# Adding the routed experts' rows: fetches that add into the residual, and scatters for the last four tiles

## What is computed

```
scores = softmax(xf @ gate_w)
_, sel = top_k(scores + expert_bias, 2)
order = argsort(sel.reshape(-1), stable=True)
token_idx = order // 2
routed_in = xf[token_idx] * top_scores_sorted[:, None]
h = silu(ragged_dot(routed_in, w1, counts)) * ragged_dot(routed_in, w3, counts)
routed_out = ragged_dot(h, w2, counts)
out = silu(xf @ sw1) * (xf @ sw3) @ sw2
out = out.at[token_idx].add(routed_out)
x = x + tanh(g_ffn[1]) * out
```

## Time and profile before

| what | us |
|---|---|
| median of 3 runs | 1395.21 |
| lowest, highest | 1388.55, 1401.52 |
| the profiled execution | 1396.1 |
| its span | 1394.4 |
| PE busy in it | 1271.6 (91%) |
| DVE, ACT, POOL busy | 652.2, 446.7, 391.7 |

### The profile page before, as it was taken

The page is one execution under the profiler, slowest core; times in us unless marked ns, Lnnn a source line. Parts: engine busy times, 40 slices in busy tenths (PEclk is TensorE's granted clock), DMA queues, the critical chain, the costliest instruction groups (busy, mean ns, idle before and its releaser), DMA issues.

```text
span 1394.4 us, 18292 instructions
## 1 busy us (share of the span) xinstructions
PE 1271.6 (91%) x6256; PEld 1073.6 (77%) x6257; DVE 652.2 (47%) x1103; ACT 446.7 (32%) x755; POOL 391.7 (28%) x327
## 2 busy tenths in 40 slices
PE   4999899999999999999999889995899999998670
PEld 3888778887888888888888778884788888887560
DVE  6555356644366646674555575563123222222116
ACT  3333342333245323531343457421122222221110
POOL 2221111000022302221334231446454310035554
PEclk9999999999999999999999999998899999999785
DMA  6821456544669845965964030435777552257647
GB/s 204 263 84 54 145 210 243 211 159 191 246 216 349 302 181 202 366 239 196 310 226 156 26 84 31 155 117 206 198 222 230 168 141 75 75 181 220 167 145 254
DMA packets 99035, 259.69 MB, mean 186 GB/s; under 512 B 8636, under 2 KB 42648, under 8 KB 86680
## 3 DMA queue, kind: packets, MB, share of 16 engines
q1 hardware_dynamic: 64824, 160.19, 32.4%
q0 software_dynamic: 33680, 98.35, 23.4%
q10 hardware_dynamic: 464, 0.27, 0.1%
HBM read 183.02 MB, written 75.76 MB: 186 GB/s over the span
## 4 chain that ended last, share of the span: by engine, by line
PE 63%; issue 14%; POOL 10%; DMA 7%; DVE 4%; another core or an unknown queue 1%; ACT 1%; POOLq 0%; ACTq 0%; DVEq 0%
PE bank L1145 25%; PE bank L1173 12%; POOL W L592 6%; PE bank L1311 6%; DMA W<-in_L_ffn_w 5%; PE bank L1070 4%; PE bank L1090 4%; PE bank L1346 2%; PE bank L1100 2%; POOL xs_sorted L732 2%; POOL fin_high L761 1%; PE bank L1117 1%; PE bank L1112 1%; DMA wdn<-in_L_ffn_W_down 1%
## 5 line engine op out<-in xcount | busy, mean ns | idle before, releaser
L1145 PE MATMUL bank<-xTh,G 128*128 128x512 f32 x1024 | 279.4, 398 | 1.8 <-DVE xTl L1592 1.8
L1145 PEld LDWEIGHTS bank<-xTh,G 128*128 128x128 f32 x1024 | 189.4, 189 | 42.8 <-issue 3.4
L1311 PE MATMUL bank<-W,dxh 128*128 (+2 forms) x880 | 204.9, 376 | 0.0
L1311 PEld LDWEIGHTS bank<-W,dxh 128*128 128x128 f32 x880 | 171.8, 195 | 15.9
L1173 PE MATMUL bank<-DN,bhh 128*128 128x512 f32 x512 | 157.9, 390 | 0.0
L1311 PE MATMUL bank<-W,dxl 128*128 (+2 forms) x440 | 117.4, 390 | 32.4 <-POOL W L592 16.4
L1145 PE MATMUL bank<-xTl,G 128*128 128x512 f32 x512 | 138.1, 392 | 0.0
L1746 DVE TENSOR_TENSOR dmid<-bank,dsg 128x448 f32<-128x448 f32 x55 | 34.3, 623 | 203.0 <-ACT dsg L954 194.7
L592 POOL TENSOR_TENSOR W<-wst,W 128x1792 fp32r<-128x1792 f32 (+1 forms) x24 | 101.4, 4226 | 87.7 <-DMA W<-in_L_ffn_w 86.3
L1614 DVE SCALAR_TENSOR_TENSOR bs<-bank,tab,bs 128x512 f32<-128x512 f32 x64 | 47.5, 743 | 160.8 <-PE bank L1145 160.8
L1346 PE MATMUL bank<-W,dhh 112*128 (+1 forms) x440 | 114.6, 403 | 0.0
(11 more groups left out here) (247 smaller groups left out, 1961.6 us busy)
## 6 DMA issues: line engine op xcount, KB each, us to landing
G<-gate_up_split SPq DMA_DIRECT2D x48, 1024.0 KB, 7.0
DN<-down_split SPq DMA_DIRECT2D x24, 1024.0 KB, 5.0
wst<-in_L_ffn_w POOLq DMA_DIRECT2D x24, 896.0 KB, 6.2
W<-in_L_ffn_w POOLq DMA_DIRECT2D x24, 896.0 KB, 7.6
gate_up_split<-G SPq DMA_DIRECT2D x16, 1024.0 KB
y_all<-dys SPq DMA_DIRECT2D x55, 256.0 KB
xs_sorted<-zero POOLq DMA_DIRECT2D x3, 3328.0 KB, 21.1
xsd<-xs_sorted SPq DMA_DIRECT2D x39, 256.0 KB, 3.3
```

Of the source, the lines that this page charges most:

```text
L1145: mm = pe.matmul(bank[m][:, :], G[:, c % 2, f, h, m, i, :], a[b % 2][:, i, :], start=(n == 0), stop=(n == 3 * DC - 1))
L1311: mm = pe.matmul(bank[o][:, 0:width], a[par][:, k, :], w[:, bass.ds(slot, 1), at + k * step:at + k * step + width].rearrange("p a n -> p ( ...
```

## The change

1. The last ADDED = 4 routed tiles (t = 51 to 54) are not stored in `y1_dram` any more. ACT writes their results into four of the row buffers (`late`), and at the very end, when all of `out` is stored, POOL adds their rows to `out` in HBM by four indirect scatters with an addition, each of which waits until the one before has landed. A row whose index is out of bounds is left out.
2. So that the rows know their token, each row of `xs1_dram` grows from 512 to 528 elements: behind the 512 stands the token's number plus one. DVE makes the numbers once (`number`), copies 16 columns of them into each row buffer before the row is normalised, and POOL scatters 528 elements. SPq reads the numbers of the last four tiles back (`late_id`), and DVE turns them into indices (`late_i`; rows that hold no token get 4095 and are out of bounds).
3. The 32 fetches of low and high rows add into `xres` themselves (`compute_op=ALU.add`) where they went to `fin_low` and `fin_high`. DVE's 32 additions go. The high fetches now wait for all the low ones. `slr` of a row in the last four tiles points into the zeros of `y1_dram`.
4. The low fetches wait for the tiles before `tlow = min(tend1[6], 35)`; the high fetches for the tiles up to t = 50.
5. The gate is multiplied in by ACT, as it takes a tile out of PSUM (`d_y`), for the shared tiles too; DVE's addition of a shared tile (L1877) becomes a plain one.

```diff
+ADDED = 4
+GATHERED = NT1 - ADDED
+ROW = D + 16
...
+        late = [rows_at[1 + i][:, 0:D] for i in range(ADDED)]
...
+            sp.dma_start(late_id[:, :], xs1_dram[GATHERED * P:NT1 * P, D:D + 1].rearrange("(k p) c -> p (k c)", p=P),
+                         allow_slow_non_contiguous=True).then_inc(s_id, 16)
...
                 load(t + 2)
-                store(t - 2)
-            for t in range(TT + NT1 - 4, TT + NT1):
-                store(t)
+                if t - 2 < TT + GATHERED:
+                    store(t - 2)
 
             for t in range(0, TT, 2):
-                sp.wait_ge(s_x4, t + 2)
+                sp.wait_ge(s_rsc[t // 2], 16 * (2 * TT // 8 + 2))
                 sp.dma_start(out_v[:, t:t + 2, :], xres[:, t:t + 2, :]).then_inc(s_out, 16)
             sp.wait_ge(s_out, 16 * TT // 2)
...
-            last = pool.value_load(tend1_i[0:1, E1 - 2:E1 - 1], min_val=1, max_val=NT1 - 1)
-            half = (last + TT + 1) // 2
+            last = pool.value_load(tlow_i[0:1, 0:1], min_val=1, max_val=GATHERED)
             for i in range(2):
-                pool.wait_ge(s_dst[i], half * 16)
+                pool.wait_ge(s_dst[i], (last + TT + 1 - i) // 2 * 16)
                 alone(None)
+            pool.wait_ge(s_sha, TT)
             for t in range(TT):
-                pool.indirect_dma_start(fin_low[:, t, :], None, y1_dram,
-                                        bass.IndirectOffsetOnAxis(ap=slr[:, 0, t:t + 1], axis=0)).then_inc(s_yg[t % 4], 16)
+                pool.indirect_dma_start(xres[:, t, :], None, y1_dram, bass.IndirectOffsetOnAxis(ap=slr[:, 0, t:t + 1], axis=0),
+                                        compute_op=ALU.add).then_inc(s_yg[t % 4], 16)
             for i in range(2):
-                pool.wait_ge(s_dst[i], 16 * ((TT + NT1 + 1 - i) // 2))
+                pool.wait_ge(s_dst[i], 16 * ((TT + GATHERED + 1 - i) // 2))
+            for i in range(4):
+                pool.wait_ge(s_yg[i], 2 * 16 * TT // 4)
             for t in range(TT):
-                if t >= 8:
-                    pool.wait_ge(s_x4, t - 7)
-                pool.indirect_dma_start(fin_high[:, t % 8, :], None, y1_dram,
-                                        bass.IndirectOffsetOnAxis(ap=slr[:, 1, t:t + 1], axis=0)).then_inc(s_rsc[t % 8], 16)
+                pool.indirect_dma_start(xres[:, t, :], None, y1_dram, bass.IndirectOffsetOnAxis(ap=slr[:, 1, t:t + 1], axis=0),
+                                        compute_op=ALU.add).then_inc(s_rsc[t // 2], 16)
+
+            pool.wait_ge(s_out, 16 * TT // 2)
+            pool.wait_ge(s_slot1, 2)
+            for j in range(ADDED):
+                pool.wait_ge(s_dy, TT + GATHERED + j + 1)
+                wait(pool, s_add, 16 * j)
+                pool.indirect_dma_start(out_rows, bass.IndirectOffsetOnAxis(ap=late_i[:, j:j + 1], axis=0), late[j], None,
+                                        bounds_check=TOK - 1, oob_is_err=False, compute_op=ALU.add).then_inc(s_add, 16)
+            pool.wait_ge(s_add, 16 * ADDED)
...
             def d_y(t):
                 act.wait_ge(s_dd, t + 1)
-                wait(act, s_dst[t % 2], 16 * (t // 2))
-                act.activation(dys[t % 2][:, :], bank[4][:, :], ACT.Copy).then_inc(s_dy, 1)
+                if t < TT + GATHERED:
+                    wait(act, s_dst[t % 2], 16 * (t // 2))
+                act.mul(dys[t % 2][:, :] if t < TT + GATHERED else late[t - TT - GATHERED], bank[4][:, :], gates[:, 3:4]).then_inc(s_dy, 1)
...
+                chain(dve.tensor_scalar(tlow[:, :], tend1[:, E1 - 2:E1 - 1], float(GATHERED), None, ALU.min))
+                chain(dve.tensor_copy(tlow_i[:, :], tlow[:, :]))
...
-                    norm(rows_at[n % 8], xres[:, t, :], t, rsc[:, k, t:t + 1]).then_inc(s_row, 1)
+                    dve.tensor_copy(rows_at[n % 8][:, D:ROW], number[:, t:t + 1].broadcast_to([P, ROW - D])).then_inc(s_row, 1)
+                    norm(rows_at[n % 8][:, 0:D], xres[:, t, :], t, rsc[:, k, t:t + 1]).then_inc(s_row, 1)
```

More of the change, by code:

```diff
@@ L98, in program @@
         gates = keep("gates", [P, 4])
-        zero = keep("zero", [P, P])
+        zero = keep("zero", [P, ROW // 4])
         reset = keep("reset", [P, E1, TT])
@@ L1774, in choice @@
             def choice():
+                chain(dve.tensor_scalar(number[:, :], cst[:, C_THR:C_THR + TT], cst[:, C_LANE:C_LANE + 1], 1.0, ALU.add, ALU.add))
                 for t in range(TT):
@@ L1876, in _ @@
                     dve.wait_ge(s_shl, 16 * (i + 1))
-                    dve.scalar_tensor_tensor(out=xres[:, i, :], in0=row[:, 0, :], scalar=gates[:, 3:4], in1=xres[:, i, :],
-                                             op0=ALU.mult, op1=ALU.add).then_inc(s_sha, 1)
+                    dve.tensor_tensor(xres[:, i, :], row[:, 0, 0:D], xres[:, i, :], ALU.add).then_inc(s_sha, 1)
+                if t == TT + 4:
+                    dve.wait_ge(s_id, 16)
+                    chain(dve.tensor_scalar(late_f[:, :], late_id[:, :], 0.0, 4096.0, ALU.is_equal, ALU.mult))
+                    chain(dve.tensor_tensor(late_f[:, :], late_f[:, :], late_id[:, :], ALU.add))
+                    chain(dve.tensor_scalar(late_f[:, :], late_f[:, :], -1.0, None, ALU.add))
+                    dve.tensor_copy(late_i[:, :], late_f[:, :]).then_inc(s_slot1, 1)
             d_hid(TT + NT1 - 1)
             dve.wait_ge(s_sha, TT)
-            for i in range(4):
-                dve.wait_ge(s_yg[i], 2 * 16 * TT // 4)
-            for t in range(TT):
-                last = dve.scalar_tensor_tensor(out=xres[:, t, :], in0=fin_low[:, t, :], scalar=gates[:, 3:4],
-                                                in1=xres[:, t, :], op0=ALU.mult, op1=ALU.add)
-            chain(last)
-            for t in range(TT):
-                dve.wait_ge(s_rsc[t % 8], 16 * (2 * TT // 8 + t // 8 + 1))
-                dve.scalar_tensor_tensor(out=xres[:, t, :], in0=fin_high[:, t % 8, :], scalar=gates[:, 3:4],
-                                         in1=xres[:, t, :], op0=ALU.mult, op1=ALU.add).then_inc(s_x4, 1)
 def shape_constants():
```

31 lines of the change are left out of this document (16 added, 15 removed).

## The result

| | before | after |
|---|---|---|
| median, us | 1393.39 (4 runs) | 1436.28 (4 runs) |
| lowest, highest | 1388.55, 1401.52 | 1434.38, 1442.96 |
| span of the profiled execution | 1394.4 | 1435.3 |
| ratio after/before, 95% | | 1.0307 (1.0268 to 1.0345) |

The changed kernel is 3.1% slower. The forecast was 1414 us with a range of 1393 to 1428: the direction was right, the size was not, and the range missed it.

What follows compares the result with a forecast made beforehand. PE was taken to dominate the chain unchanged, with POOL's pace and the DMA engines bounding the end. Low fetches 1331.2 to 1359.4, high fetches and stores to 1400.1, scatters to 1412.9 (+18.5): median 1414 us, range 1393 to 1428.

Steps and rivals of the forecast that it cites:

- The stages ahead: Everything before the low fetches: small DVE values and copies ahead of POOL's row scatters add 1.2 us, the rest nothing.
- zeros and numbers: Fill of `xs1_dram`, read of `late_id`, small DVE operations: hidden, 0; the fill under 2 us if its cover went.
- later than 1334: row stage: Sign in the profile after: a first low fetch later than 1334 us means the row tiles' preparation and scatters cost more.
- Row stage: DVE's copies ahead of POOL's row-tile scatters: +0.5 us within a sum of +1.2; as a rival, +6, chance 0.05.
- The start of the low fetches: At the end, low fetches wait for the store of t = 50, not t = 51: 8.57 us earlier.
- The fetches that add: Low and high fetches at the end: each costs 1.58 us of all DMA engines, 0.90 plain plus 0.68 for reading `xres`.
- double or more: Rival on the end's adding fetches: at 1.81 us each the whole takes 1421 us, at 2.7 near 1450; chance 0.15.
- Additions are free: Rival on the end's adding fetches: the second read hides inside POOL's 1.26 us pace, giving 1397 us; chance 0.35.
- 11 us of waiting: Waiting removed at the end: high fetches could start near 1353 rather than 1364 if fetches cost what they did.
- The scatters: Four final scatters in a row, first 3.6 us, others 2.9 each: 12.3, plus 0.2 wait and 0.3 to the span's end.

Runs made afterwards that it cites:

- wide fill: Changed kernel with the zeros of `xs1_dram` written in whole rows of 2112 bytes, not pieces of 528: 1419.38 us, ratio 1.0240.
- late `number`: Changed kernel with DVE making `number` behind the mask that PE waits for, not at the head of `choice`: 1425.04 us, ratio 1.0269.
- both mendings: Changed kernel with the fill in pieces of 2112 bytes and `number` made later on DVE, together: 1413.97 us, ratio 1.0180.

## Why the forecast was right in direction and short in size

*The stages ahead, forecast +1.2.* The first trace had +12.4, the next of the same kernel less: its low fetches start at 1333.28, and the three kernels without the wider rows (1335.50, 1330.89, 1332.63), each less the 8.57 that the change takes from the wait, would start at 1322.3 to 1326.9. So it is 6 to 11 us there, and the traces with the wide fill, alone (1321.39) and with the late `number` (1321.21), have nothing of it left.
- The first step that failed is "zeros and numbers": "the fill of `xs1_dram` is 3% larger and goes while PE is busy", "under 2 us". I counted bytes. The change divides the longer row by four and so makes pieces of 528 bytes, 1.6 times as dear each MB. The cover was the DMA's spare 17 and 30%; it is used up (1.02), and PE's transfers come late. In the first profile that was little, PE short by 0.93 us in 400 to 490; in the four other traces with this fill PE waits 2.7 to 6.1 us for `vnat`, and the rank matmuls start 6 us later in the mean than with the wide fill. The waits lower the clock too: in the windows with waits of 1.93, 2.55, 2.67, 4.63 and 4.67 us the granted clock is 0.91 to 0.97, with those of 0.78 and 1.47 it is 1.00.
- `number` was priced at its own length, 0.2 (it takes 0.23). The price is on PE: the hole ahead of the rank matmuls grows from 1.58 to 1.93 us, the clock falls to its lower level, 32 matmuls take 6.03 and not 3.63 us, and the first scatter comes 4.2 us later. In five profiles with a hole of 1.89 to 1.93 us the clock fell in four; in nine with 1.58 to 1.66 in none. The exception is the kernel with the wide fill alone (1.93, then 3.63), so the longer hole makes it likely and not certain. Mended alone it gave 2.7 us of the median, within the noise.
- Of the first trace's 12.4, the clock is 4.2, the small values ahead of the first scatter 0.5 and PE's waits for the fill 0.9. The rest, some 7, is that execution against before's: 1.2 ahead of the rank matmuls, 2.7 in the row stage, 3.0 behind it, and what held it is not known. By its own sign ("later than 1334: row stage") the forecast was wrong here, but the copies that it meant were not the cause.
- "Row stage", +0.5 for the copies (bounds 0 and 7.6): nothing in seven of the eight profiles with copies. The 49.8 us of the first trace, which would have spoken for a loss of 2.7, is that execution's own. The small values and the first copy ahead of it, priced 0.4 and 0.1, measured 0.5.

*The start of the low fetches, 8.57 us earlier.* Right: with both mendings they start at 1321.21, 9.7 to 14.3 before those of the three kernels that keep the old wait.

*The fetches that add, forecast 1.58 us of the engines, measured 1.80.* This is the second step that failed, a term that was too small: it took the nearest row for the second read and missed by 14%. The rival "double or more" had the price: 2 x 0.90. The Trainium skill's two reads on one ring ("Collectives: The Full Stack", section on why ReduceScatter is half of AllGather) say so of the reductions of collectives, and the trace of the low half agrees: 1.80 us. Beside the stores of `out` it is 1.50, where a plain fetch had 0.483 x 17 / 10.2 = 0.80, a factor of 1.9. But the low half took 34.2 us and not the 31.8 of that rival, because of a term that neither had: POOL's own issue of such a fetch is 1.54 us, so its pace of 1.26 became 1.85, just over what the engines need. The last fetch starts 27.9 us after the first, lands 5.6 later, and 0.7 passes until POOL goes on. I had used POOL's pace as a constant from the earlier trace rows. The high half came out at 38.9 for 40.8: right as a sum, with 1.50 and 0.70 for the forecast's 1.58 and 0.68. POOL kept its pace up to 1404.34, and with the engines full the last data landed 7.65 us later.

*"Additions are free", 0.35.* Shown wrong by the adding fetches alone: +20 us with all the rest as before. Its argument was 0.36 us of slack in POOL's pace; the second read needs 0.90, and the pace moved too.

*"11 us of waiting" that the change takes away.* They were 8.57 and 5.87 us, less what the high fetches now wait for the low ones. The 8.57 was there in every trace with the old wait (8.55 to 8.57). The 5.87, the high fetches' wait for the last store, was one execution's; the fetches of other executions follow each other without it. To read a "remote" release as the kernel's own was the error; it cost the forecast little, since the high half was worked out from its own start.

*The scatters, forecast 12.6 with the end, measured 19.8.* The third step that failed: four round trips priced too short, and the end behind them at nearly nothing. An empty one lands after 2.7 us as the earlier trace rows said, but POOL goes on only 0.8 us later: 3.5 each and not 2.9. The first, with 74 rows and their addition, takes 5.6 and not 3.6. And behind the last one the span goes on for 7.1 us, of which 2.7 are its landing, if it lands as the two before it; I had taken 2.9 and 0.3. Before, SPq's last wait and the end were 0.3 us apart; here 4.4 us lie between. Every kernel with scatters has it (7.1 to 7.2 behind the last one, in all seven that have four). Whether it comes from the engine that issued and waited, or from the kind of transfer, no run tells.

The sum by experiment, from 1388 us, each against the kernel before on its own chip: adding fetches +20 (alone), scatters and end +20 (their row of waits), stages ahead +6 to +11, start of the low fetches -8.6: 37 to 42, and the changed kernel's later run was +40. In the first measurement it was +43, and the some 3 us more are not explained.

## What to carry to other kernels

An addition in the DMA is not free and not only the engines' affair: price its second read as a whole second fetch, and look at what the issuing engine takes for it. When a row's length changes, look for every transfer that divides it, because the size of the pieces can matter far more than the bytes. And ask of each small operation on a helper engine who is waiting behind it: 0.23 us on DVE cost the way to the first scatter 4.2 us through PE's clock, in four profiles of five. One trace is one execution: the first profile here had 14 us in two stages that the same kernel did not have again.

## What the runs showed of the hardware

- An indirect fetch of 128 x 2 KB with an addition takes 1.80 us of the 16 DMA engines (plain 0.90) and 1.54 us of POOL (plain 0.95). Beside direct stores of 0.70 us each it took 1.50 of the engines (plain 0.80).
- A scatter of 128 rows that are all out of bounds takes 3.5 us from its start to POOL's next one when it is waited for.
- Filling with pieces of 528 bytes took 69 us of an engine for each MB; 2112 bytes took 43 and 512 bytes 44 (each in a window with other traffic of the queue in it).
- After a hole of 1.9 us in PE's work the granted clock went to its lower level for about 10 us in four of five profiles, and in none of nine after 1.6 us. Each of the four had 17.2 us from there to the first scatter, the others with the same work 13.0.
- An indirect fetch of POOL was held for 8.4 and 8.9 us beside twelve additions of DVE in two kernels, ending 0.82 us behind the twelfth both times, and not at all beside sixteen in another.
- Between the landing of the last scatter, which POOL waits for, and the program's end lay 4.4 us (its landing taken as 2.7 us, like the others'); behind the last store that SPq waits for it was 0.3.
